# A recommender tower on one core: a new order of the work of a chunk, and a second table of 1,250 rows on chip, looked up in three chunks of eight

## The reference

```python
e = jnp.stack([tbl_0[ids[:, 0]], ..., tbl_25[ids[:, 25]]], axis=1)      # 2048 x 26 x 128
combined = jnp.concatenate([dense[:, None, :], e], axis=1)              # 27 vectors
inter = jnp.einsum('bnd,bmd->bnm', combined, combined)[:, triu_i, triu_j]
h = jnp.concatenate([dense, inter, dense], axis=1)                      # 607 columns
h = jnp.maximum(h @ W_top1 + b_top1, 0.0)                               # 512
h = jnp.maximum(h @ W_top2 + b_top2, 0.0)                               # 256
y = h @ W_top3
```

## Time and profile before

| | |
|---|---|
| median of three runs | 371.46 us |
| profiled execution | 371.68 us |
| its span, first to last instruction | 369.8 us |
| around the span | 1.88 us |
| PE busy | 331.2 us (90%) |
| POOL busy | 259.1 us (70%) |
| DVE busy | 208.4 us (56%) |
| ACT busy | 188.2 us (51%) |
| mean granted clock of TensorE | 0.991 of full speed |

### The profile page before, as it was taken

How to read it: one execution, slowest core, us unless ns; L and a number is a source line. 1 busy time by engine, 2 the same in 40 slices (tenths; PEclk the granted TensorE clock), 3 DMA queues, 4 the chain that set the end, 5 groups by cost and what they waited for, 6 DMA issues and landing times.

```text
span 369.8 us, 13491 instructions
## 1 busy us (share of the span) xinstructions
PE 331.2 (90%) x6048; PEld 295.2 (80%) x6048; DVE 208.4 (56%) x376; ACT 188.2 (51%) x222; POOL 259.1 (70%) x280
## 2 busy tenths in 40 slices
PE   0486759899999999999999989998999989999797
PEld 0476747898899889997899769996889868997676
DVE  3799925792289506980398406980289505960031
ACT  2698643356355664556365554555445552555402
POOL 6777777777777777777777777777777777777100
PEclk9999998999999999999999999999999999999989
DMA  7999527672236512672247322572236512542330
GB/s 178 249 256 206 159 69 236 141 228 56 60 78 171 169 51 62 124 232 60 54 96 194 127 58 54 125 241 51 58 85 158 176 52 53 110 111 59 77 47 14
DMA packets 49332, 44.24 MB, mean 120 GB/s; under 512 B 33359, under 2 KB 39094, under 8 KB 49274
## 3 DMA queue, kind: packets, MB, share of 16 engines
q1 hardware_dynamic: 39166, 25.36, 27.4%
q0 software_dynamic: 8704, 17.84, 18.0%
q10 hardware_dynamic: 1404, 0.17, 0.3%
HBM read 37.91 MB, written 5.44 MB: 117 GB/s over the span
## 4 chain that ended last, share of the span: by engine, by line
PE 78%; DMA 8%; POOL 4%; issue 4%; SPq 2%; ACT 2%; DVE 0%; DVEq 0%
PE banks L449 37%; PE banks L472 13%; PE mlp L492 8%; PE moved L431 8%; PE mlp L502 7%; DMA hidden<-in_tbl_dram 6%; POOL rows L404 4%; DMA rows<-in_tbl_dram,ids_sb 3%; SPq L253 2%; PE banks L538 1%; PE mlp L514 1%; PE banks L552 1%; ACT vectors L866 1%; ACT vectors L849 1%; PE mlp L538 1%
## 5 line engine op out<-in xcount | busy, mean ns | idle before, releaser
L404 POOL DMA_INDIRECT rows<-in_tbl_dram,ids_sb x272 | 258.1, 949 | 83.9 <-issue 80.2
L711 DVE TENSOR_TENSOR masks<-hot_ids,row_of 125x512 fp32r<-125x512 int32 (+1 forms) x336 | 186.4, 619 | 59.9 <-PE banks L449 51.6
L449 PE MATMUL banks<-masks,high 125*128 125x256 f32 x592 | 152.4, 296 | 16.7 <-DVE low L698 16.7
L449 PE MATMUL banks<-masks,low 125*128 125x256 f32 x592 | 147.2, 287 | 0.0
L449 PEld LDWEIGHTS banks<-masks,high 125*128 125x128 f32 x592 | 115.6, 195 | 17.7 <-issue 14.6
L449 PEld LDWEIGHTS banks<-masks,low 125*128 125x128 f32 x592 | 115.9, 196 | 0.0
L866 ACT ACTIVATE vectors<-moved 128x512 f32<-128x512 f32 (+1 forms) x79 | 86.5, 1094 | 22.6 <-PE moved L431 22.6
L849 ACT ACTIVATE vectors<-banks 128x512 f32<-128x512 f32 (+1 forms) x40 | 44.4, 1110 | 70.4 <-PE banks L449 70.4
L472 PEld LDWEIGHTS banks<-vectors 128*27 128x27 f32 x4096 | 45.6, 104 | 22.6 <-issue 14.8
L472 PE MATMUL banks<-vectors 128*27 128x27 f32 x4096 | 56.3, 193 | 4.7 <-issue 3.7
L431 PE MATMUL moved<-identity,rows 128*128 128x128 f32 x271 | 45.0, 281 | 14.1 <-ACT vectors L866 6.4
(11 more groups left out here) (49 smaller groups left out, 65.4 us busy)
## 6 DMA issues: line engine op xcount, KB each, us to landing
hot_ids<-in_ids_of_field_dram SPq DMA_DIRECT2D x32, 256.0 KB, 4.7
rows<-in_tbl_dram,ids_sb POOLq DMA_INDIRECT x272
features<-scratch SPq DMA_DIRECT2D x7, 351.0 KB
scratch<-products SPq DMA_DIRECT2D x56, 42.2 KB
scratch<-products SPq DMA_DIRECT2D x28, 81.2 KB
w_sb<-in_tbl_dram SPq DMA_DIRECT2D x3, 448.0 KB
hot_ids<-in_ids_of_field_dram SPq DMA_DIRECT2D x8, 128.0 KB
dense_sb<-in_dense_dram SPq DMA_DIRECT2D x8, 128.0 KB, 5.3
```

Source lines behind the costliest of these rows:

```text
L404: pool.indirect_dma_start(rows[:, (tile * TILE_ROWS + v) % RING, :], None, tables[f][:, :], bass.IndirectOffsetOnAxis(ap=ids_sb[:, tile, f ...
L449: last = nc.tensor.matmul(banks[:, j % BANKS, m * CHUNK:(m + 1) * CHUNK], part[:, part_of(j * PAIR + m, k), :], masks[:, mask % MASK_RING, ...
L711: nc.vector.tensor_tensor(masks[:, mask % MASK_RING, 0:size], hot_ids[0:PART_ROWS, n % ID_RING, 0:size], row_of[0:PART_ROWS, row:row + 1]. ...
```

## The change

- **A second table of 1,250 rows on chip** (`SOMETIMES`, loaded by SP in front of the weights into a place of its own; ACT rounds and copies it in chunk 1, and DVE's `split(HOT)` stands ahead of `sum_weights` and of the last masks of chunk 1). Its field is looked up in chunks 3, 5 and 7, where pair 4 has two fields (10 masks of double width, 40 matmuls), and there the fifth batch of each tile, which holds that field alone, is left out: no gather, no `turn(a,4)`, no `turn(b,4)`. In the other five chunks the field is gathered. Gathers: 272 before, 266 now.
- **A new order of a chunk.** Pair 1 of the next chunk is looked up in the chunk before, too: `look_up(i+1,0)` whole behind `turn(b,2)`, and `look_up(i+1,1)` in four pieces, one ahead of `turn(b,4)` and three among the products of the second tile. `first_layer(i-1,0)` stands ahead of `turn(a,4)`, and the two visits of `multiply(i,1)` and the second layer stand ahead of `turn(b,2)`. ACT's and DVE's orders follow (`place_dense` behind the masks of pair 1).
- **The first chunk** has the same pattern: its steps are taken visit by visit.
- **The end**: the last batch is transposed through `moved` and copied by ACT as the others are (before, its single row had a bank of its own and DVE); the second layer and `last_layer` of chunk 6 stand ahead of the last products; `multiply(LAST,3)` stands behind two of the four `first_of_half(0, m)`; SP's `store_y(LAST-1)` stands ahead of the writes of the second half.

The core of the diff (helpers that only count batches and rows with the shorter tiles, and declarations, are cut):

```diff
+LOOKED_UP = (3, 5, 7)
+ONE_HOT = [SOMETIMES, ALWAYS] + SHORTS
+STAGED = SHORTS + [ALWAYS, SOMETIMES]
...
-TILE_ROWS = len(GATHERED)
+TILE_ROWS = len(GATHERED) + 1
...
+def batches_of(t):
+
+    return TILE_BATCHES - (t // TILES in LOOKED_UP)
+
+def fields_of(c, j):
+
+    if j < HOT_PAIRS - 1:
+        return (PAIR * j, PAIR * j + 1)
+    return (HOT, HOT - 1) if c in LOOKED_UP else (HOT - 1,)
...
             load_dense(1)
+            load_table(HOT)
...
             load_last(0)
+            store_y(LAST - 1)
             write_last(1)
-            store_y(LAST - 1)
             load_last(1)
...
-                for b in range(TILE_BATCHES):
+                for b in range(batches_of(tile)):
                     gather(tile, b)
...
             def end():
-                first_layer(LAST - 1, 0)
                 multiply(LAST, 0, (0,))
-                turn(b, 0)
                 first_layer(LAST - 1, 1)
                 multiply(LAST, 0, (1,))
-                turn(b, 1)
+                turn(b, 0)
                 multiply(LAST, 1, (0,))
                 first_layer(LAST - 1, 2)
                 multiply(LAST, 1, (1,))
+                turn(b, 1)
+                first_layer(LAST - 1, 3)
+                second_layer(LAST - 1, 0)
                 turn(b, 2)
-                first_layer(LAST - 1, 3)
-                second_layer(LAST - 1, 0, range(0, 2))
+                second_layer(LAST - 1, 1)
                 turn(b, 3)
-                second_layer(LAST - 1, 0, range(2, MTILES1))
+                last_layer(LAST - 1)
                 turn(b, 4)
-                second_layer(LAST - 1, 1, range(0, 2))
                 multiply(LAST, 2)
-                multiply(LAST, 3)
-                second_layer(LAST - 1, 1, range(2, MTILES1))
-                last_layer(LAST - 1)
                 first_of_half(0, 0, every)
                 first_of_half(0, 1, every)
+                multiply(LAST, 3)
                 first_of_half(0, 2, every)
...
             def first_chunk():
                 turn(1, 1)
-                multiply(0, 0)
+                multiply(0, 0, (0,))
                 turn(1, 2)
-                multiply(0, 1)
+                multiply(0, 0, (1,))
                 turn(1, 3)
+                multiply(0, 1, (0,))
+                look_up(1, 0, range(0, 3))
+                multiply(0, 1, (1,))
+                look_up(1, 0, range(3, PARTS[0]))
                 turn(1, 4)
+                look_up(1, 1, range(0, 2))
+                products_of_second_tile(0)
...
                 make_masks(i, 0)
+                make_masks(i, 1)
                 place_dense(i)
-                make_masks(i, 1)
                 keep_dense(i - 1)
                 for j in range(2, HOT_PAIRS):
                     if i == 1 and j == HOT_PAIRS - 1:
+                        split(HOT)
                         sum_weights()
...
             def chunk(i):          # ACT
                 keep_batch(a, 0)
-                keep_pair(i, 1)
+                keep_pair(i, 2)
+                if i == 1:
+                    round_table(HOT)
+                    copy_table(HOT)
...
                 keep_batch(a, 3)
-                keep_pair(i, 4)
+                keep_first(i - 1, 0)
                 keep_batch(a, 4)
...
                 keep_batch(b, 2)
+                keep_pair(i + 1, 0)
                 keep_batch(b, 3)
                 keep_batch(b, 4)
                 keep_step(i, 2)
                 keep_step(i, 3)
+                keep_pair(i + 1, 1)
```

More of the change, by code:

```diff
@@ L52 @@
 PAIR = BANK // CHUNK
-HOT = len(ONE_HOT)
+HOT = len(STAGED) - 1
 HOT_PAIRS = -(-HOT // PAIR)
 WIDTHS = [min(PAIR, HOT - PAIR * j) for j in range(HOT_PAIRS)]
-PARTS = [ROWS[ONE_HOT[PAIR * j]] // PART_ROWS for j in range(HOT_PAIRS)]
+PARTS = [ROWS[STAGED[PAIR * j]] // PART_ROWS for j in range(HOT_PAIRS)]
 FIRST_PART = [sum(WIDTHS[n] * PARTS[n] for n in range(j)) for j in range(HOT_PAIRS + 1)]
@@ L97, in batch_of_row @@
 def batch_of_row(g):
-    tile, v = divmod(g, TILE_ROWS)
-    return tile * TILE_BATCHES + max(b for b in range(TILE_BATCHES) if tile_batch(b)[0] <= v)
+    tile = max(t for t in range(ALL_TILES) if rows_before(t) <= g)
+    v = g - rows_before(tile)
+    return batches_before(tile) + max(b for b in range(TILE_BATCHES) if tile_batch(b)[0] <= v)
 def part_of(h, k):
@@ L173, in build @@
         dense_loaded = [sem(f"dense_loaded{n}") for n in range(2)]
-        table_loaded = [sem(f"table_loaded{n}") for n in range(HOT)]
+        table_loaded = [sem(f"table_loaded{n}") for n in range(HOT + 1)]
         weights_loaded = sem("weights_loaded")
@@ L397, in gather @@
             def gather(tile, b):
-                last = tile * TILE_ROWS + tile_batch(b)[-1]
+                last = rows_before(tile) + tile_batch(b)[-1]
                 if last >= RING:
@@ L422, in turn @@
                     return
-                n = t * TILE_BATCHES + b
+                if b >= batches_of(t):
+                    return
+                n = batches_before(t) + b
                 batch = tile_batch(b)
-                pe.wait_ge(rows_loaded[t % TILES * TILE_BATCHES + b], (t // TILES + 1) * 16 * len(batch))
-                own = t == ALL_TILES - 1 and b == TILE_BATCHES - 1
-                if n and not own:
+                loads = sum(b < batches_of(n) for n in range(t % TILES, t + 1, TILES))
+                pe.wait_ge(rows_loaded[t % TILES * TILE_BATCHES + b], loads * 16 * len(batch))
+                if n:
                     pe.wait_ge(batch_kept, n)
-                place = banks[:, LAST_ROW_BANK, :] if own else moved
                 for m, v in enumerate(batch):
-                    last = nc.tensor.transpose(place[:, m * TILE:(m + 1) * TILE],
-                                               rows[:, (t * TILE_ROWS + v) % RING, :], identity[:, :])
+                    last = nc.tensor.transpose(moved[:, m * TILE:(m + 1) * TILE],
+                                               rows[:, (rows_before(t) + v) % RING, :], identity[:, :])
                 last.then_inc(batch_ready, 1)
@@ L436, in look_up @@
                 ks = ks or range(PARTS[j])
+                if c == min(LOOKED_UP) and j == HOT_PAIRS - 1:
+                    pe.wait_ge(low_made, HOT + 1)
                 if c == 0:
@@ L643, in chunk, with products_of_second_tile @@
+                products_of_second_tile(0)
+            def products_of_second_tile(i):
+                multiply(i, 2, (0,))
+                look_up(i + 1, 1, range(2, 4))
+                multiply(i, 2, (1,))
+                look_up(i + 1, 1, range(4, 6))
+                multiply(i, 3, (0,))
+                look_up(i + 1, 1, range(6, PARTS[1]))
+                multiply(i, 3, (1,))
             def chunk(i):
-                a = TILES * i
+                a, b = TILES * i, TILES * i + 1
                 turn(a, 0)
-                look_up(i, 1)
+                look_up(i, 2)
@@ L661, in end_of_chunk @@
                 multiply(i, 0, (0,))
-                turn(b, 0)
                 first_layer(i - 1, 1)
                 multiply(i, 0, (1,))
-                turn(b, 1)
+                turn(b, 0)
                 first_layer(i - 1, 2)
                 multiply(i, 1, (0,))
+                first_layer(i - 1, 3)
+                multiply(i, 1, (1,))
+                turn(b, 1)
+                second_layer(i - 1, 0)
+                second_layer(i - 1, 1)
                 turn(b, 2)
-                first_layer(i - 1, 3)
+                look_up(i + 1, 0)
@@ L683, in _ @@
             pe.wait_ge(constants_made, CONSTANTS)
             first_chunk()
-            second_chunk()
-            for i in range(2, CHUNKS):
+            for i in range(1, CHUNKS):
                 chunk(i)
@@ L1029, in end_of_last @@
+                keep_first(LAST - 1, 3)
                 keep_batch(b, 2)
-                keep_first(LAST - 1, 3)
+                keep_second(LAST - 1, 0)
                 keep_batch(b, 3)
-                keep_second(LAST - 1, 0)
+                keep_batch(b, 4)
             first_chunk()
-            second_chunk()
-            for i in range(2, CHUNKS):
+            for i in range(1, CHUNKS):
                 chunk(i)
```

152 lines of the change are left out of this document (58 added, 94 removed).

## The result

The changed kernel takes 404.11 us (median of 4 runs, 402.80 to 405.01), the kernel before 371.5: a ratio of 1.0869 [1.0845, 1.0892]. It is 8.7% slower, where the prediction said 5% (390 us, range 377 to 399): the direction was right, the size lies above the range. The profiled span is 403.2 us, in place of 388.5 in the prediction's sum.

A forecast was written before the change was run, and what follows sets the result against it. POOL set the pace from chunk 4, PE having under 2 us a chunk to spare. First chunk 63.5 + chunks 1 to 6 268.5 + rest 56.5 = 388.5 us, with 1.9 around it 390.4; forecast 390, range 377 to 399.

The forecast's parts named there:

- Bound and direction: Whole kernel: POOL sets the pace before, PE is the later of the two after the change; 390 us, 5% slower.
- (2): Fifth batch of tile a: products wait for ACT's copy, 1.0 us in chunks 1, 2, 4 and 6, 0.3 in looked-up chunks.
- (3): End of tile b: PE waits for ACT's copies, 1.8 us in a normal chunk, 1.1 in a looked-up one.
- Place (1): Ahead of first_layer(i-1,0): PE waits for the products' load, 1.8 us in chunks 1, 2, 4, 6; 0.1 in 3 and 5.
- under the cover of this wait: Chunk 1, DVE's split(HOT): PE waits about 2 us, but the load of Place (1) would hold it as long anyway.
- the one clear gain, some 6 us: First chunk: chunk 1 begins at 63.5 with pair 1 already looked up, where before it began at 63.6.
- I let both go: PE's gaps of 1.97 us (first chunk) and 1.96 us (the end) vanish, visits being spread among longer matmuls.
- The early load of the table: Start of the kernel: the table's 640 KB are loaded before PE is through chunk 0, at no cost.
- The end: Last chunk: the write and load of the second half set the end; 56.5 us, where it had 55.4.
- C: Rival for the whole kernel: the load lands as late as the bound allows and PE's gaps stay; 402 us, chance 0.06.
- A: Rival: waits are covered (under about 3 us over six chunks) and the change pays; 367.5 us, chance 0.10.

The follow-up runs named there:

- kernel 2: The changed kernel's new order without the second table, its field gathered in all chunks (272 gathers): 400.70 us, ratio 1.0792.
- kernel 3: The changed kernel with pair 4 and pair 0 each cut in two around a transpose, so ACT's copies run under look-ups: 388.95 us, ratio 1.0492.
- kernel 4: The changed kernel with the second table loaded behind the weights instead of ahead of them: 399.91 us, ratio 1.0781.
- kernel 6: The changed kernel with both the edits of kernel 3 and the later table load of kernel 4: 386.68 us, ratio 1.0404.
- kernel 1: The kernel before plus the second table and its look-ups in chunks 3, 5 and 7, with the old order on all engines: 379.35 us, ratio 1.0245.
- kernel 7: The changed kernel with 112 matmuls that nobody reads put on PE ahead of its waits in chunks 1 to 6: 397.64 us, ratio 1.0691.
- kernel 9: kernel 6 with turn(a,2) put into pair 3, the cut of pair 4 moved, and more masks between the products' visits: 382.85 us, ratio 1.0305.

## Why the prediction was right in direction and too small in size

**Bound and direction: right.** POOL gave up the pace, PE waits at all three places, and the order alone costs 7.9% (kernel 2).

**Places (2) and (3): right.** Forecast 1.0 us at (2), measured 0.72 to 0.83 in the normal chunks and 0.11 to 0.12 in the looked-up ones (0.3 forecast): 3.4 us in all, 4.6 forecast. At (3) 1.08 to 1.10 + 0.51 (1.8 forecast) and 1.00 (1.1): 8.4 us, 9.4 forecast. Covered, they are nearly gone (kernel 3).

**Place (1): mis-sized.** The sum had 4 x 1.8 + 2 x 0.1 = 7.4 us; the waits were 0.37, 0.61, 1.87 and 1.01 in chunks 1, 2, 4 and 6 and none in 3 and 5, 3.9 us. Timeline of SP and PE in chunks 1 and 2:

```profile
80.73 0.30 SPq L321 DMA_DIRECT2D features<-scratch  x1
...
84.78 2.00 PE L529 MATMUL mlp<-features,w_sb 117*128 117x256 f32 x8 [0.37 <-DMA features<-scratch]
...
126.20 0.30 SPq L321 DMA_DIRECT2D features<-scratch  x1
...
129.74 2.00 PE L529 MATMUL mlp<-features,w_sb 117*128 117x256 f32 x8 [0.61 <-DMA features<-scratch]
```

From its issue to PE's going on the load took 4.05 us in chunk 1, and 3.54, 4.00 and 3.45 in 2, 4 and 6, where 3.7 was forecast: that estimate was good. An estimate of 2.8 us from the figures of the Trainium skill ("DMA: Bandwidth & Descriptors", the anatomy of one DMA), which are for DMAs of GpSimd, is further off. PE came as early as forecast in chunks 2, 4 and 6, 12.7 us after the products (12.5). Chunk 4 had the forecast's wait; in 2 and 6 the load was issued 9.8 and 10.3 us after them (10.6 forecast) and landed sooner. In chunk 1 PE was late, held up by the masks of pair 4 and a copy; the prediction had put about 2 us there under the cover of this wait, and it was 1.9.

**The first chunk: the step that failed most.** The prediction counted "the one clear gain, some 6 us". Chunk 1 began at 70.09 in place of 63.5, 4.2 us later than before with 3.9 us of work less to do: no gain. 1.2 us of the miss lie ahead of the first products, which began at 46.76 (the sum starts at 45.6, as before). From there to chunk 1 it took 23.3 us where 17.9 were forecast. "I let both go, as visits are now spread among longer matmuls" was wrong: gaps of 3.35 and 0.21 us stand there, and the clock behind the first was at 1.2 GHz for some 5 us, which took about 2. Without the table (kernel 2) or with the load later (kernels 4 and 6), the same stretch in the same order takes 18.7, 20.0 and 19.5 us, with 1.0, 2.2 and 1.8 us of gaps. Less these it is 17.6 to 17.9: the work was summed rightly, and the gaps put at nothing, with the clock behind them, are the whole miss of that stretch.

**What the gaps are.** The trace has a DMA queue for instructions (from the page of the changed kernel: queue, kind, packets, MB, share of 16 engines):

```profile
q8 instruction: 48, 0.79, 0.8%
```

These are 48 transfers of 16 KB, one for each 257 of the 12,348 records of PE (matmuls, weight loads, semaphores). Behind the first products the 14 profiled executions have 91 gaps of PE with no releaser, 0.16 to 4.45 us. Two, of 0.71 and 0.20 us ahead of a transpose, are put down to ACT in other runs. The other 89 all stand at the same place of a run of 256 records (193 or 194 records behind a multiple of 256, counted from PE's first), and each ends 1.2 to 1.8 us after one of these transfers has landed. That of the 3.35 us ran from 51.84, when PE had stood since 50.90, to 52.97, and PE went on at 54.25. So in these gaps PE waits for its next block of instructions (that the transfers are PE's is read from their number). A block lasts PE 1.3 us in products (64 records of matmul in 0.67) and 15 in look-ups (0.12 apiece), which is why longer matmuls between the visits help.

The early load of the table, costed at nothing, delays such a block. The transfer for the crossing at 50.90 started 4.7 us after PE had crossed into the block before it; in kernels 1, 3 and 7, with the early load, too, it was 4.5, 4.0 and 3.3, in the ten kernels without it 1.0 to 1.6. PE stood there for 3.35, 4.45, 2.73 and 2.37 us with the early load and at most 1.40 without. The Trainium skill ("Runtime: NRT & Kernel Launch", the mechanics of instruction fetch) says that the cost of crossing an instruction block is mostly hidden. Most of the 48 crossings of a run agree; the 2 to 13 of a run that are these gaps do not. The prediction had weighed this mechanism, and two of the three gaps that the kernel before has (the third, 1.36 us, is the one up to 49.93), and put them at nothing.

**Chunks 1 to 6: two terms were missing.** 242.7 + 4.4 for the look-ups + 3.9 + 3.4 + 8.4 for the places + 1.1 of waits for masks and a copy in chunk 1 make 263.9; measured were 276.2. Of the 12.3 us left, 4.7 are gaps without a releaser (eight of 0.22 to 0.99 us), and the clock takes 5.8 (PE's busy time less that of kernel 3). The 1.8 left are in part pair 4 in chunk 1, whose masks came 0.33 us apart in place of 0.24 (0.8 us); the rest stays unplaced. The prediction had the gaps only at two places, as a risk, and the clock not at all: it priced each wait at its own length, where behind three of them PE ran the next 3 to 7 us at half clock. How much the clock takes differs between runs: the profiled execution has the lowest mean clock of the four (0.966 and 405.01 us), the shortest the highest (0.983 and 402.80).

**The end: right** (56.5 forecast, 56.9 measured), with the load of the second half setting it.

**Rivals.** C's 402 us came nearest, by half of its mechanism and so in part by luck: the gaps stayed, but the waits for the load were shorter, not longer. A was wrong because its condition, waits under about 3 us, was missed by far; kernel 9, the nearest to it of those in the new order, still has PE idle for 6.1 us in the chunks (254.8 - 248.7) and is slower than before.

## What to carry to other kernels

A wait of TensorE can cost more than its length: look at the granted clock behind every wait of a microsecond in the trace, and put long matmuls there even if they must be taken from elsewhere. A gap of TensorE with no releaser in a run of very short matmuls can be a wait for instructions: set it beside the transfers of the instruction queue. Keep such runs apart with long matmuls, and keep large loads that nobody needs yet out of them. When work is handed from one full engine to another, start with the smallest amount that moves the pace: one chunk looked up gained 0.4%, two with a mended first chunk 1.2%, three under the same old order lost 0.8%.

## What the runs showed of the hardware

- The granted clock fell to its 1.2 GHz level behind a wait of 1.87 us (0.50 from 224 to 230), and matmuls went at half their pace behind waits of 1.10 and 0.51 us in chunk 2; it stayed at 1.00 behind waits of 1.08 and 0.51 us in chunk 4, and in chunks filled with matmuls that nobody reads. The Trainium skill ("TensorE: Matmul & The Clock Gate", Part 1) says that how busy the engine has lately been decides between the two levels; the filled kernel agrees.
- In runs of products TensorE stopped for up to 4.45 us with no releaser, in the middle of a visit (after 35 of 64 records, after 40 of 128, after 48 of 64). Such stops, 89 in the 14 traces with some ahead of a look-up or a transpose, all stand at one place of a run of 256 of its records and end 1.2 to 1.8 us after a transfer of 16 KB on the instruction queue has landed: TensorE waited for instructions. With 640 KB loaded at that time the transfer for one such place started 3.3 to 4.7 us behind the crossing before it, without that 1.0 to 1.6.
- Extra work was better than free here: 13 us of matmuls that nobody reads made a kernel 6.5 us faster.
